# Normalization work moved from VectorE to ScalarE in an attention and gated-mixing layer, with a new order for the last tiles

## What is computed

```python
x = x + layernorm(attention(layernorm(x)))      # one head of width 256
x = x + layernorm(mixing(layernorm(x)))

def attention(x):       # x @ weight_qkv partly in float16 (64 columns at either end)
    q, k, v = split(x @ weight_qkv)
    s = softmax(q @ k.T / sqrt(256))
    return (s @ v) @ out_w.T + out_b

def mixing(x):
    prev = x shifted down by one row, a row of zeros ahead of each batch
    xr = mu_r * x + (1 - mu_r) * prev
    xk = mu_k * x + (1 - mu_k) * prev
    return sigmoid(xr @ W_r.T) * (square(relu(xk @ W_k.T)) @ W_v.T)
```

## Time and profile before

| | |
|---|---|
| median of 3 runs | 833.16 us (830.95 to 833.72) |
| the profiled execution | 831.39 us, of which the span of the trace 829.6 us |
| PE busy | 782.6 us (94%) |
| DVE busy | 759.6 us (92%) |
| ACT busy | 510.0 us (61%) |
| POOL busy | 479.8 us (58%) |

### The profile page before, as it was taken

The page is one execution under the profiler, slowest core; times in us unless marked ns, Lnnn a source line. Parts: engine busy times, 40 slices in busy tenths (PEclk is TensorE's granted clock), DMA queues, the critical chain, the costliest instruction groups (busy, mean ns, idle before and its releaser), DMA issues.

```text
span 829.6 us, 16266 instructions
## 1 busy us (share of the span) xinstructions
PE 782.6 (94%) x5765; PEld 568.3 (69%) x5765; DVE 759.6 (92%) x1822; ACT 510.0 (61%) x631; POOL 479.8 (58%) x692
## 2 busy tenths in 40 slices
PE   4879999999999998999999998999999999998983
PEld 3436677777767775777776775777777777777872
DVE  5698989999999999999999999999999999899895
ACT  3375555676666665667656666666766667665453
POOL 2210255577656566576655766656776576567674
PEclk9999999999999999999999999999999999999998
DMA  7565777587757585756676755747767465458301
GB/s 183 115 152 109 152 170 142 122 160 141 155 87 160 124 175 118 146 132 119 158 127 152 151 132 119 160 90 160 140 140 141 105 113 115 108 122 185 83 26 52
DMA packets 365090, 108.69 MB, mean 131 GB/s; under 512 B 338768, under 2 KB 364752, under 8 KB 365008
## 3 DMA queue, kind: packets, MB, share of 16 engines
q1 hardware_dynamic: 365008, 107.64, 62.4%
HBM read 18.75 MB, written 8.39 MB: 33 GB/s over the span
## 4 chain that ended last, share of the span: by engine, by line
PE 61%; DVE 32%; issue 4%; POOL 1%; DMA 1%; SPq 1%; ACT 0%; DVEq 0%; POOLq 0%
DVE p_lo L1010 7%; DVE probs L994 6%; PE S L1308 5%; PE S L1309 5%; PE S L1310 5%; PE S L1312 5%; PE S L1311 5%; PE Y L1329 4%; PE Y L1332 4%; PE Y L1330 4%; PE Y L1331 4%; PE Y L1333 4%; PE M L1276 4%; PE M L1278 4%; PE M L1277 4%
## 5 line engine op out<-in xcount | busy, mean ns | idle before, releaser
L994 DVE TENSOR_SCALAR_CACHE_REDUCE probs<-S 128x512 f32<-128x512 f32 x256 | 172.9, 676 | 18.2 <-PE S L1312 18.2
L745 ACT ACTIVATE probs<-probs,exp_bias,kappa 128x2048 f32<-128x2048 f32 x64 | 134.0, 2093 | 82.7 <-DVE exp_bias L1005 82.0
L1010 DVE TENSOR_TENSOR p_lo<-probs,p_hi 128x2048 f16<-128x2048 f32 x64 | 175.1, 2736 | 2.0 <-ACT p_hi L695 1.9
L1329 PE MATMUL Y<-pt_hi,planes 128*128 128x256 f16 x496 | 135.4, 273 | 0.0
L1330 PE MATMUL Y<-pt_lo,planes 128*128 128x256 f16 x496 | 135.3, 273 | 0.0
L1331 PE MATMUL Y<-pt_hi,planes 128*128 128x256 f16 x496 | 135.3, 273 | 0.0
L1332 PE MATMUL Y<-pt_lo,planes 128*128 128x256 f16 x496 | 135.3, 273 | 0.0
L1333 PE MATMUL Y<-pt_hi,planes 128*128 128x256 f16 x496 | 135.3, 273 | 0.0
L695 ACT ACTIVATE p_hi<-probs 128x2048 f16<-128x2048 f32 x64 | 121.4, 1897 | 18.4 <-DMA pt_lo<-p_lo 18.3
L1308 PE MATMUL S<-turned,q_hi 128*128 128x512 f16 x256 | 97.8, 382 | 15.2 <-DVE q_lo L985 12.1
L1309 PE MATMUL S<-turned,q_lo 128*128 128x512 f16 x256 | 97.8, 382 | 0.0
(11 more groups left out here) (208 smaller groups left out, 2047.9 us busy)
## 6 DMA issues: line engine op xcount, KB each, us to landing
x_res<-in_L_attn_x SPq DMA_DIRECT2D x32, 256.0 KB, 3.1
out_x<-gate SPq DMA_DIRECT2D x32, 256.0 KB, 2.2
xs<-in_L_attn_x SPq DMA_DIRECT2D x28, 128.0 KB, 3.0
xs<-in_L_attn_x SPq DMA_DIRECT2D x14, 256.0 KB, 3.4
pt_hi<-p_hi SPq DMA_TRANSPOSE x62, 4.0
pt_lo<-p_lo SPq DMA_TRANSPOSE x62, 4.0
mxt<-mx SPq DMA_TRANSPOSE x27, 3.3
pt_hi<-in_L_attn_weight_qkv SPq DMA_DIRECT2D x3, 128.0 KB, 3.1
```

Of the source, the lines that this page charges most:

```text
L994: dve.tensor_scalar(probs[:, h % 2, t, c * BLK:(c + 1) * BLK], S[k % RING][:, :], 1.0, None, ALU.mult, ALU.max, accum_out=chunk_max[:, t, ...
L1010: dve.tensor_tensor(p_lo[:, t, :], probs[:, h % 2, t, :], p_hi[:, t, :], ALU.subtract).then_inc(p_lo_made, 1)
L1329: pe.matmul(to[:, 0, :], low, p_h, start=first, stop=False, skip_group_check=True)
```

## The change

- The two row norms that DVE did in the loop as (x - mean) * rstd leave it: `mix_in` (now `mix_norm`) and `pre_norm` for batches 1 to 3 go to ACT, as x * rstd + shift, with shift = -mean * rstd made by two more small POOL instructions each time. The norms of the very first batch stay on DVE.
- The multiplication of the inverse sums by `top[:, OUT]` is gone. In its place the bias row and the eps of the norm behind it are divided by that factor, once, in `scales` on POOL; the layer norm cancels the factor.
- `carry` goes from POOL to ACT, into a slot of its own (47).
- The stages from `res_rsqrt` to `differences` are one slot later (the norm itself two), `mix` stays where it was. Preparation starts two slots later, and its low part and transposition are one slot earlier in relation to it.
- DVE's `residual_stats`, POOL's `res_rsqrt` and POOL's `pre_rsqrt` now wait in the loop for the norm of the tile (or group) before.
- The lists of the drain are new on all engines. PE's is shown; on DVE one `mix_in`, one `attention_norm`, two `gate_norm` and two `split_low` fewer stand in it, and four `finish` more; POOL's `carry`s are gone; ACT has a list with `mix_norm` of H-3 and H-2, `attention_norm` of H-3 to H-1, `gate_norm` of H-7, H-6, H-4, H-3 and H-2, and the `carry`s.

```diff
-    RES_RSQRT = 39
-    MIX_IN = 39
-    MIX_HIGH = 40
-    MIX_LOW = 41
-    TURN_MIX = 42
-    DIFF = 45
+    RES_RSQRT = 40
+    MIX_NORM = 41
+    MIX_HIGH = 41
+    MIX_LOW = 42
+    TURN_MIX = 43
+    DIFF = 46
+    CARRY = 47
...
-    PREP, PREP_EVERY = 18, 12
-    PREP_LOAD, PREP_STATS, PREP_RSQRT, PREP_NORM, PREP_HIGH, PREP_LOWER, PREP_TURN = -8, 0, 1, 2, 4, 6, 7
+    PREP, PREP_EVERY = 20, 12
+    PREP_LOAD, PREP_STATS, PREP_RSQRT, PREP_NORM, PREP_HIGH, PREP_LOWER, PREP_TURN = -8, 0, 1, 2, 4, 5, 6
...
             def pre_rsqrt(n):
                 i = n % 2
                 pool.wait_ge(pre_moments, (n + 1) * NT)
+                if n >= NJ + 2:
+                    pool.wait_ge(pre_normed, (n - 1) * NT)
                 pool.tensor_scalar(pvar[:, i, :], pmv[:, i, :, 1], EPS, 2.0 ** (-2 * X_EXP), ALU.add,
                                    ALU.mult).then_inc(pre_eps, 1)
+                if n >= NJ:
+                    pool.tensor_scalar(pminus[:, i, :], pmv[:, i, :, 0], -1.0, 0.0, ALU.mult, ALU.add).then_inc(pre_turned, 1)
                 pool.wait_ge(pre_eps, n + 1)
                 pool.tensor_tensor(prstd[:, i, :], pvar[:, i, :], minus_half[:, :], ALU.pow).then_inc(pre_rstd, 1)
+                if n >= NJ:
+                    pool.wait_ge(pre_turned, n - NJ + 1)
+                    pool.wait_ge(pre_rstd, n + 1)
+                    pool.tensor_tensor(pshift[:, i, :], pminus[:, i, :], prstd[:, i, :], ALU.mult).then_inc(pre_shift_made, 1)
...
+                pool.tensor_scalar(bias_row[:, :], bias_row[:, :], inv_top[:, OUT:OUT + 1], 0.0, ALU.mult,
+                                   ALU.add).then_inc(bias_scaled, 1)
+                pool.tensor_tensor(att_part[:, :], inv_top[:, OUT:OUT + 1], inv_top[:, OUT:OUT + 1],
+                                   ALU.mult).then_inc(att_part_made, 1)
+                pool.wait_ge(att_part_made, 1)
+                for t in range(RT):
+                    pool.tensor_scalar(att_eps[:, t:t + 1], att_part[:, :], EPS, 0.0, ALU.mult, ALU.add).then_inc(att_eps_made, 1)
...
-                pool.tensor_tensor(avar[:, :], amv[:, :, 1], eps[:, :], ALU.add).then_inc(a_eps_added, 1)
+                pool.tensor_tensor(avar[:, :], amv[:, :, 1], att_eps[:, :], ALU.add).then_inc(a_eps_added, 1)
...
-            def res_rsqrt(h):
+            def res_rsqrt(h, shifts):
                 pool.wait_ge(r_moments, (h + 1) * RT)
                 if h == 0:
                     pool.wait_ge(scales_made, 3 + RT)
-                if h >= LEFT:
+                if h >= 1:
                     pool.wait_ge(mix_in_made, h * RT)
                 pool.tensor_scalar(rvar[:, :], rmv[:, :, 1], EPS, mix_shrink[:, 1:2], ALU.add, ALU.mult).then_inc(r_eps_added, 1)
+                if shifts > 0:
+                    pool.tensor_tensor(rminus[:, :], zeros[:, :], rmv[:, :, 0], ALU.subtract).then_inc(r_mean_turned, 1)
                 pool.wait_ge(r_eps_added, h + 1)
                 pool.tensor_tensor(rrstd[:, :], rvar[:, :], minus_half[:, 0:RT], ALU.pow).then_inc(r_rstd_made, 1)
+                if shifts > 0:
+                    pool.wait_ge(r_rstd_made, h + 1)
+                    pool.wait_ge(r_mean_turned, shifts)
+                    pool.tensor_tensor(rshift[:, :], rminus[:, :], rrstd[:, :], ALU.mult).then_inc(r_shift_made, 1)
...
-            def carry(h):
-                if h >= TURN_LEFT:
-                    pool.wait_ge(xt_made, h + 1)
-                if h >= 1:
-                    pool.wait_ge(mixed_made[0], h * HALVES)
-                    pool.wait_ge(mixed_made[1], h * HALVES)
-                if (h + 1) % PER == 0:
-                    pool.memset(xt[:, (h + 1) % 2, :, 0:1], 0.0).then_inc(carried, 1)
-                else:
-                    pool.tensor_copy(xt[:, (h + 1) % 2, :, 0:1], xt[:, h % 2, :, ROWS:ROWS + 1]).then_inc(carried, 1)
...
+            def pre_norm(n):
+                i = n % 2
+                act.wait_ge(pre_shift_made, n - NJ + 1)
+                for t in range(NT):
+                    o = rows_of(n)[:, t, :]
+                    act.activation(o, o, ACT.Identity, bias=pshift[:, i, t:t + 1],
+                                   scale=prstd[:, i, t:t + 1]).then_inc(pre_normed, 1)
...
+            def mix_norm(h, shifts):
+                act.wait_ge(r_shift_made, shifts)
+                for t in range(RT):
+                    act.activation(att[:, h % 2, t, :], res[:, h % 4, t, :], ACT.Identity, bias=rshift[:, t:t + 1],
+                                   scale=rrstd[:, t:t + 1]).then_inc(mix_in_made, 1)
...
+            def carry(h):
+                act.wait_ge(xt_made, h + 1)
+                if h >= 1:
+                    act.wait_ge(mixed_made[0], h * HALVES)
+                    act.wait_ge(mixed_made[1], h * HALVES)
+                if (h + 1) % PER == 0:
+                    copy(xt[:, (h + 1) % 2, :, 0], zeros[:, :]).then_inc(carried, 1)
+                else:
+                    copy(xt[:, (h + 1) % 2, :, 0], xt[:, h % 2, :, ROWS]).then_inc(carried, 1)
...
             def inverse_sums(h):
                 dve.wait_ge(exp_made, (h + 1) * RT)
-                dve.reciprocal(inv_sum[:, h % 4, :], row_sum[:, h % 4, :]).then_inc(sum_inverted, 1)
-                dve.wait_ge(sum_inverted, h + 1)
-                dve.tensor_scalar(inv_sum[:, h % 4, :], inv_sum[:, h % 4, :], top[:, OUT:OUT + 1], None,
-                                  ALU.mult).then_inc(inv_made, 1)
+                dve.reciprocal(inv_sum[:, h % 4, :], row_sum[:, h % 4, :]).then_inc(inv_made, 1)
 
             def attention(h):
                 dve.wait_ge(inv_made, h + 1)
                 dve.wait_ge(o_done, h + 1)
+                if h == 0:
+                    dve.wait_ge(bias_scaled, 1)
...
                 dve.wait_ge(r_stats, (h + 1) * RT)
-                if h >= LEFT:
+                if h >= 1:
                     dve.wait_ge(mix_in_made, h * RT)
                 dve.sem_inc(waited, 1)
...
-                if (h := at(k, MIX_IN)) is not None:
-                    mix_in(h)
...
-                if (n := prep(k, PREP_NORM)) is not None:
-                    pre_norm(n)
...
+            values(H - 3, 1, 2)
+            project_out(H - 4, KEYS_LEFT)
+            values(H - 3, 2, 7)
+            receptance(H - 6)
+            feed(H - 7)
             turn_mix_in(H - 5)
-            project_out(H - 4, KEYS_LEFT)
-            values(H - 3, 1, 5)
             mix_keys(H - 6, 0)
-            values(H - 3, 5, 8)
-            receptance(H - 6)
-            values(H - 2, 0, 2)
+            values(H - 3, 7, 8)
+            values(H - 2, 0, 3)
+            feed(H - 6)
             project_out(H - 3, KEYS_LEFT)
-            values(H - 2, 2, 4)
+            values(H - 2, 3, 4)
+            mix_keys(H - 5, 0)
+            values(H - 2, 4, 8)
             turn_mix_in(H - 4)
-            values(H - 2, 4, 5)
-            feed(H - 7)
-            values(H - 2, 5, 8)
-            feed(H - 6)
+            values(H - 1, 0, 1)
             receptance(H - 5)
             project_out(H - 2, KEYS_LEFT)
-            mix_keys(H - 5, 0)
-            values(H - 1, 0, 5)
+            feed(H - 5)
+            values(H - 1, 1, 3)
+            mix_keys(H - 4, 0)
             turn_mix_in(H - 3)
-            feed(H - 5)
-            mix_keys(H - 4, 0)
-            values(H - 1, 5, 8)
+            values(H - 1, 3, 8)
+            feed(H - 4)
+            project_out(H - 1, KEYS_LEFT)
             turn_mix_in(H - 2)
             receptance(H - 4)
-            project_out(H - 1, KEYS_LEFT)
             mix_keys(H - 3, 0)
-            feed(H - 4)
             receptance(H - 3)
+            feed(H - 3)
             mix_keys(H - 2, 0)
-            feed(H - 3)
+            turn_mix_in(H - 1)
             receptance(H - 2)
-            turn_mix_in(H - 1)
             feed(H - 2)
             mix_keys(H - 1, 0)
             receptance(H - 1)
```

In ACT's drain list the last attention norm now stands here:

```diff
+            receptance(H - 4)
+            squares(H - 3)
+            attention_norm(H - 1, H - 1)
             split_high(H - 2, 1)
```

More of the change, by code:

```diff
@@ L870, in _ @@
[L870 to L872 removed]
+            carry(H - 4)
             receptance(H - 5)
[L874 to L879 removed]
+            split_high(H - 4, 1)
+            mix_norm(H - 3, H - 4)
+            attention_norm(H - 2, H - 2)
+            squares(H - 4)
+            mix_in_out(H - 3)
```

205 lines of the change are left out of this document (106 added, 99 removed).

## The result

| | median | lowest to highest | profiled execution | its span |
|---|---|---|---|---|
| before, the same 4 rounds | 833.02 us | 830.95 to 833.72 | 831.39 us | 829.6 us |
| changed | 818.71 us | 817.83 to 819.64 | 817.83 us | 816.0 us |

The ratio is 0.983, with a 95% interval from 0.981 to 0.985: 14.3 us faster. The forecast was 815.6 us with a range from 811.0 to 822.5, from a sum of 17.6 us of gain, where 14.3 came.

A forecast was written before the change was run, and what follows sets the result against it. DVE bounds the stretches with preparation, PE the others, the drain is mixed. From 831.39 us, -11.0 - 1.4 - 4.2 - 1.0 = -17.6 gives 813.8; with 1.8 for the median, 815.6 us, range 811 to 822.5.

The forecast's parts named there:

- the loop: Tiles with preparation: DVE's relief, several times the excess, brings them to PE's floor of 23.70 us a tile; 11.0 us gained.
- the head: Between 30 and 70 us, PE's 3.7 us of waits for q_lo shrink; 1.4 us gained, between 0 and 3.7.
- up to the last projection: First part of the drain: new lists have every operand ready ahead of its matmul; 4.2 us gained, between 0 and 4.9.
- The bound from below: Loop: with multiplies at 0.23 us each, 1.8 instead of 8.6 us, DVE's relief is still 22.0 us.
- ScalarE: Loop: taking the norms and `carry`, ACT goes from 126.0 to about 147 of 189.6 us, covered by its idle time.
- Rival B: Loop: ACT is late with the preparation's norm ahead of q_hi, so the 11.0 us stay lost; 826.6 us, chance 0.05.
- POOL gets lighter: Loop: POOL loses `carry`, 11.7 us over eight tiles, and gets small instructions of 6.5 us; nothing on the path.
- C: Rival, loop: differences come over 5.4 us later and DVE waits at `mix` on every tile; 854.6 us, chance 0.03.
- D: Rival, loop: DVE's other instructions slow by as much, so only the drain gains; 828.0 us, chance 0.03.
- behind the last projection: End of the drain, 31.4 us before: norm and differences of the last tile; -1.0 us, between +2 and -3.
- the cover of the turn: Behind the last projection: a split of 0.7 us, hidden by the turn, replaces what held the last differences by 1.2 us.
- Rival A: Drain: the new lists give nothing, as one late operand shifts all behind it; 820.8 us, chance 0.22.

The follow-up runs named there:

- the frame: Kernel before and changed kernel, each with plain DMAs in place of its 171 DMA transposes: 832.04 us and 819.89 us.
- the factor alone: Kernel before with plain DMAs, VectorE's multiply of the inverse sums taken out, bias row and eps on GpSimd answering for the factor: 821.01 us, ratio 0.986.
- The run that cut the wait of 2.35 us: Changed kernel with plain DMAs, GpSimd's `split_low(H - 3, 0)` moved ahead of `att_rsqrt(H - 1, H - 1)` in the drain: 819.25 us, ratio 0.983.

## Why the prediction was right or wrong

The profiled executions lie 13.6 us apart, and the sum's four terms account for it: 11.0 in the loop, 1.3 in the head, 1.75 up to the last projection, and -0.4 behind it, where 11.0, 1.4, 4.2 and 1.0 were forecast.

**Right: the loop.** 11.0 us expected, 11.0 found, and for the reason given: VectorE was in arrears, and TensorE's 23.70 us a tile is the floor. "The relief is several times the excess" was right too; each of two parts of it is enough alone. The bound from below was too careful in one thing: the multiply's 8.6 us were to shrink to 1.8 if its waiting passed on, and by itself this part took 11.1 us from VectorE (186.95 to 175.86), its own 8.6 and 3.6 of `p_lo`, whose mean fell from 2830 to 2604 ns. It was GpSimd that got busier: its list in the loop is the same in that version, and it was busy for 135.4 us instead of 127.9. VectorE ended at 157.4, below the 160 to 166 expected, since its mixes got shorter too (699 to 541 ns, 5.1 us a batch). A part of the 11.0 us went through the clock, which the prediction didn't look at: behind the 2.63 us wait the kernel before had a granted clock of 0.50:

```profile
316.80:320.10 3.30, 3.12 (x10) 1.49 (x11) 3.30 (x4) 2.31 (x4) 2.19 (x3) 0.50 0.01 2
```

That is some 1.7 us of TensorE's time, an estimate from that share over 3.3 us. The changed kernel has 1.00 in both stretches.

**Right in number, not shown in mechanism: the head.** Tile 10 starts 1.3 us earlier (217.94 to 216.65), 1.4 expected, and 1.4 earlier in the frame. But the waits for q_lo that were to shrink grew from 3.7 to 4.3 us, and those for `probs`, for which the step had no term, fell from 3.1 to 1.5. The start of tile 10 lies between 216.5 and 221.0 us in the profiled executions of all versions, so the agreement is luck in part.

**Right: ScalarE.** 144.4 us a batch where 147 were expected, with the copy at 0.198 instead of 0.3. Rival B had no place: TensorE waits for no q_lo behind 70 us. The norms took 593 and 588 ns there, where VectorE had taken 653 and 604. The advice against adds and multiplies on ScalarE, in the Trainium skill, ScalarE: Activation LUTs, Rules for kernel authors, gives VectorE's speed per element in bf16 as its reason; these norms are float32, and for them it isn't borne out.

**Wrong in sign, at no cost: GpSimd.** "POOL gets lighter": 125.1 became 136.0 us a batch. The 1678 ns of `carry` were mostly VectorE's `p_lo`: 0.25 us is what the copy takes away from it. In the changed kernel the final adds meet `p_lo` instead. Those that start inside one take 2.77 or 2.78 us and the others 0.72 to 0.91; their mean is 1590 ns in the stretch, where it was 754. `carry`'s leaving is not the whole of it, though: with the factor alone, and `carry` in place, GpSimd was as busy (135.4). The step priced instructions, and not whom they would meet. TensorE waited for none of it in the loop.

**Not seen: C and D.** VectorE waited 1.0 us in the whole run for GpSimd's differences, and the relief came in full.

**Wrong in size: "walked through with the durations above, every operand is there ahead of its matmul up to the last projection", -4.2 us.** It was -1.75. One operand was not there: the 3.34 us wait for H-6's low parts is the only one of over 0.25 us up to the last projection, and 47.25 less 3.34 is 43.9, where the walk without waits had 44.1. The walk had no term for ScalarE's wait for a landing ahead of that tile's splits. The experiment that swaps them gets back 1.4 of the 2.4 us there and 2.3 in the median.

**Wrong in size: behind the last projection, -1.0 us.** It was +0.4, within the bounds of +2 and -3. The attention norm began 5.13 us behind the projection's end, 5.3 expected. Then the differences started at 798.05, 13.9 behind it, as before (13.8), and took 0.9 longer, and the mixes 0.8. Those 1.7 are nearly all of the 1.8 by which the keys came later behind the projection (18.7 against 16.9), and the runs show both: `sq_lo` holds the diff when it starts first, and the final adds of H-3 hold the mixes. The step had no term for either, though the earlier trace rows had shown the effect; it took "the cover of the turn" for a cover in time alone. The gate norm that had held the differences by 1.2 us is gone, as expected: they start 0.04 us behind their input. But the mix input's norm ahead of them started 11.7 us behind the projection, where it was 10.5 before. GpSimd's and VectorE's rows, of before and then of after:

```profile
807.61 0.70 POOL L526 TENSOR_TENSOR rrstd<-rvar,minus_half 128x2 f32<-128x2 f32 x1
...
808.74 0.73 DVE L1059 TENSOR_SCALAR att<-res,rmv,rrstd 128x256 f32<-128x256 f32 x2
```

```profile
792.59 1.16 POOL L613 TENSOR_TENSOR xm_lo<-mixed,xm_hi 128x512 f16<-128x512 f32 x1
...
794.08 0.69 POOL L551 TENSOR_TENSOR rrstd<-rvar,minus_half 128x2 f32<-128x2 f32 x1
...
794.08 0.69 DVE L1126 SCALAR_TENSOR_TENSOR gate<-rec,S 128x512 f32<-128x512 f32 x1 [0.85 <-PE S L1323]
794.80 0.75 DVE L1132 BATCH_NORM_STATS2 gst<-gate 128x6 f32<-128x256 f32 x2
795.89 0.75 DVE L1110 TENSOR_SCALAR att<-res,rmv,rrstd 128x256 f32<-128x256 f32 x2
```

The norm's rrstd is ready 0.5 us later behind the projection (10.6 against 10.1), most of it since a subtraction of GpSimd's stands ahead of it in the new list. The other 0.7 come behind that: `gated_stats(H - 3)`, which the old list has behind this norm, stands ahead of it in the new one, and its gate had waited 0.85 us for TensorE. That is a reading of two traces; no run moved these places alone. The run that cut the wait of 2.35 us didn't bring the 1.2 us back, as its attention norm came 0.6 us later. In return the last stretch, from the keys to the end, fell from 14.3 to 13.0 us.

Rival A (820.8, the drain gives nothing) had 0.22. The truth lies between it and the forecast, nearer A for the drain's part: 1.3 of 5.2 us in the profiled executions.

## What to carry to other kernels

When one engine is a few per cent over the bound of another, any one relief somewhat larger than the excess brings the whole gain, and the next brings nothing (in the first eight tiles 5.2 us brought 3.2 of 5.1, 6.9 brought all, and 29 no more than that): before making five edits, work out how much must go, take somewhat more (a third more was enough here), and stop there. An instruction of a few elements that takes a microsecond shows its neighbour's time; on an engine that doesn't meet that neighbour it takes its own, but on the engines left behind other instructions meet instead. Two engines that share an interface need a term in the sum wherever they meet, in the tail above all. In a hand-written tail look at what each engine has ready while it waits, and before moving an instruction later, ask which buffer its result sets free.

## What the runs showed of the hardware

- A copy of 128 x 2 took 0.198 us on ScalarE (seven, 197 to 207 ns). The same copy on GpSimd took 0.25 us in two cases and 2.25 us in the five that started inside VectorE's `p_lo`.
- A VectorE multiply of 128 x 2 beside a GpSimd subtraction ended with it: 1.08 us in all eight tiles, 0.23 at 72.90 us, with GpSimd idle.
- GpSimd's busy time in tiles 10 to 18 rose from 127.9 to 135.4 us when nothing but a VectorE multiply was taken out of the loop.
- TensorE's granted clock fell around waits of 3.42 and 3.01 us (to 0.77 over 10 us and 0.58 over 5, shares of 2.4 GHz with 1.2 as the lower level). It did not behind 3.34 in the changed kernel, and in the head the same wait of 2.26 us was followed by 0.83 in one execution and 1.00 in another: the length of a wait alone doesn't tell it.
- Plain DMAs of a head's probabilities, 512 KB each, landed in 5.2 (high) and 6.8 us (low) at the median in the changed kernel and in 3.8 and 5.0 in the kernel before; the transposes of the same bytes in 4.9 and 4.8, and in 4.0 and 4.0. The transpose was at most 0.2 us slower, and for the low parts faster.
